# New instruction orders for a one-layer vision transformer on one core

## The reference

```python
h = layernorm(p, ln1_g, ln1_b)                         # p: patches, 1152 x 768
h = layernorm(einsum('bsd,dm->bsm', h, W) + b, ln2_g, ln2_b)   # 192 wide
# attention: 12 heads of 16; each of the 36 patch positions attends over the 32 images
q, k, v = split(norm(h) @ in_proj_weight.T + in_proj_bias)
o = softmax(normalize(q) @ normalize(k).T * exp(min(logit_scale, 4.605))) @ v
h = h + (o * head_scale) @ out_w.T + out_b
# gated FFN with 8-bit activations and 3-valued weights
up, gate = split(bitlinear(norm(h), w_in, g_in))        # 512 each
h = h + bitlinear(silu(gate) * up, w_out, g_out)
```

## Time and profile before

| | |
|---|---|
| median of three runs | 125.61 us (125.09 to 126.04) |
| profiled execution | 125.35 us |
| its span, first to last instruction | 123.5 us |
| busy in the span: PE, DVE, ACT, POOL | 114.8, 104.6, 78.9, 74.6 us |
| mean granted TensorE clock | 0.993 of full speed |
| DMA | 7.68 MB, nearly all of it in the first 35 us |

### The profile page before, as it was taken

One profiled execution on the slowest core, in us unless ns is written; L12 is line 12 of the kernel. 1 busy time (PEld: TensorE's weight loads), 2 busy tenths in 40 slices (PEclk: granted clock), 3 DMA queues, 4 the chain that ended last, 5 costly groups with the idle time before them and its releaser, 6 DMA issues.

```text
span 123.5 us, 4889 instructions
## 1 busy us (share of the span) xinstructions
PE 114.8 (93%) x1940; PEld 95.3 (77%) x1948; DVE 104.6 (85%) x338; ACT 78.9 (64%) x179; POOL 74.6 (60%) x172
## 2 busy tenths in 40 slices
PE   6999999999999998999999979999999999999970
PEld 6989998797997986887867748599686787687850
DVE  0488984899999999799997999999999999998820
ACT  0405356676898555692856948678679587999730
POOL 7100167555446451193782777998887999999800
PEclk9999999999999999999999999999999999999997
DMA  3999978899910000000000000000000000111111
GB/s 90 255 194 178 182 140 163 150 180 222 310 53 0 5 0 5 5 0 5 3 5 0 5 0 5 0 5 5 0 5 3 5 0 16 47 43 53 48 50 49
DMA packets 24509, 7.68 MB, mean 62 GB/s; under 512 B 20579, under 2 KB 23909, under 8 KB 24486
## 3 DMA queue, kind: packets, MB, share of 16 engines
q1 hardware_dynamic: 21732, 6.92, 26.7%
q10 hardware_dynamic: 2754, 0.45, 2.6%
HBM read 6.48 MB, written 0.88 MB: 60 GB/s over the span
## 4 chain that ended last, share of the span: by engine, by line
PE 65%; POOL 10%; DVE 10%; issue 5%; ACT 5%; DVEq 0%; POOLq 0%
PE bank L750 11%; PE bank L772 8%; PE bank L773 7%; PE bank L796 6%; PE bank L784 5%; PE bank L650 4%; PE bank L654 3%; POOL yw L449 3%; PE bank L730 2%; PE bank L761 2%; PE bank L813 2%; PE bank L668 2%; PE bank L814 2%; PE bank L661 2%; PE bank L830 2%
## 5 line engine op out<-in xcount | busy, mean ns | idle before, releaser
L750 PE MATMUL bank<-w_emb_c,xT 128*128 128x192 f32 x108 | 19.3, 329 | 0.0
L654 PE MATMUL bank<-ones 128*128 128x128 f32 x126 | 19.2, 284 | 0.0
L750 PEld LDWEIGHTS bank<-w_emb_c,xT 128*128 128x128 f32 x108 | 17.3, 190 | 0.2
L654 PEld LDWEIGHTS bank<-ones 128*128 128x128 f32 x126 | 16.2, 191 | 1.0 <-issue 0.9
L381 POOL TENSOR_TENSOR rs<-mv,mhalf 128x1 f32<-128x1 f32 x9 | 5.2, 586 | 15.3 <-DVE mv L957 15.3
L772 PE MATMUL bank<-w_qkv,xhT 97*128 97x384 f32 (+1 forms) x36 | 12.0, 415 | 0.9 <-DVE qkp L1026 0.8
L773 PE MATMUL bank<-w_qkv,xhT 96*128 96x384 f32 (+1 forms) x36 | 11.7, 405 | 0.0
L449 POOL TENSOR_TENSOR yw<-yy,gout_bc 128x512 f32<-128x512 f32 x8 | 10.2, 1270 | 0.2 <-POOL yy L438 0.2
L796 PEld LDWEIGHTS bank<-vx,pT 32*32 32x32 f32 x864 | 8.5, 104 | 2.1 <-issue 1.9
L796 PE MATMUL bank<-vx,pT 32*32 32x17 f32 x864 | 9.3, 181 | 0.8 <-issue 0.8
L772 PEld LDWEIGHTS bank<-w_qkv,xhT 97*128 97x128 f32 x36 | 6.2, 189 | 4.1 <-issue 1.6
(11 more groups left out here) (173 smaller groups left out, 336.5 us busy)
## 6 DMA issues: line engine op xcount, KB each, us to landing
xs<-in_x_dram SPq DMA_DIRECT2D x32, 96.0 KB, 3.5
out_dram<-h_all SPq DMA_DIRECT2D x34, 24.0 KB, 1.5
wi_raw<-in_L_ffn_w_in_dram SPq DMA_DIRECT2D x1, 768.0 KB, 6.4
w_emb_sb<-in_L_tok_W_dram SPq DMA_DIRECT2D x2, 288.0 KB, 3.3
w_qkv_raw<-attn_in_proj_weight_dram SPq DMA_DIRECT2D x1, 432.0 KB
xs<-in_x_dram ACTq DMA_DIRECT2D x4, 96.0 KB, 5.0
wo_raw<-in_L_ffn_w_out_dram SPq DMA_DIRECT2D x1, 384.0 KB, 5.0
gout_bc<-in_L_ffn_g_out_dram SPq DMA_DIRECT2D x1, 256.0 KB, 7.6
```

What stands on the lines that cost most here:

```text
L654: nc.tensor.matmul(bank[b][:, 3 * P:4 * P], ones[:, :], ones[:, :], start=True, stop=True)
L750: mm = nc.tensor.matmul(emb_bank, xT[:, t % 3, P * k:P * (k + 1)], w_emb_c[:, 3 * (k % 2) + k // 2, :], start=(k == 0), stop=(k == KF - 1))
```

## The change

Four of the five orders are written anew: GpSimd's, ScalarE's, TensorE's and VectorE's lists; SyncE's stays. The same steps run as before, with these exceptions: tile 4's up part goes by upc(4) on ScalarE and yyp(4) on GpSimd in place of yy_(4) on VectorE; tile 7's weighting is ywd(7) on VectorE in place of yw_(7) on GpSimd; 60 spare calls in place of 63; some extra waits of calls are named differently, and ms2_ loses its own. Diff lines that only reorder steps of which nothing below speaks are left out.

```diff
@@ -46,10 +46,10 @@
...
-WEIGHED_ON_DVE = (8,)
-WEIGHED_ON_POOL = (0, 1, 2, 3, 4, 5, 6, 7)
-UP_COPIED = (0, 1, 2, 3)
-UP_READ = (4, 5, 6, 7, 8)
+WEIGHED_ON_DVE = (7, 8)
+WEIGHED_ON_POOL = (0, 1, 2, 3, 4, 5, 6)
+UP_COPIED = (0, 1, 2, 3, 4)
+UP_READ = (5, 6, 7, 8)
@@ -467,18 +467,18 @@
...
-nw_(4); nv_(4); an4_(0); an4_(1); wfac_(); f_h_(0); rs3_(6); f_h_(1); rs3_(7); rs2_(8); nm3_(6); hg_(8); nw_(5)
-nv_(5); rs3_(8); e5_(0); yyp(0); yw_(0); s4_(2); s4_(3); nm3_(7); nm3_(8); an4_(2); nw_(6); nv_(6); e5_(1)
-f_h_(2); an4_(3); e5_(2); ms5_(0); yyp(1); f_h_(3); yw_(1); s5_(0); an5_(0); yyp(2); ms5_(1); s5_(1); nw_(7)
-nv_(7); ms5_(2); s5_(2); s4_(4); yw_(2); an5_(1); s4_(5); yyp(3); f2_(0); an5_(2); an4_(4); f_h_(4); f2_(1)
-nw_(8); nv_(8); s4_(6); an4_(5); f_h_(5); e5_(3); ms5_(3); e5_(4); e5_(5); yw_(3); s5_(3); an4_(6); yw_(4)
-f2_(2); an5_(3); ms5_(4); f_h_(6); yw_(5); f2_(3); s5_(4); ms5_(5); s4_(7); e5_(6); s5_(5); an4_(7); f_h_(7)
-yw_(6, (yq_ok, 4)); s4_(8); ms5_(6); s5_(6); an4_(8); an5_(4); e5_(7); f2_(4); f_h_(8); yw_(7); ms5_(7); s5_(7)
-an5_(5); f2_(5); e5_(8); an5_(6); an5_(7); f2_(6); f2_(7); ms5_(8); s5_(8); an5_(8); f2_(8)
...
+nv_(4); wfac_(); f_h_(0); rs3_(6); nm3_(6); s4_(1); s4_(2); rs3_(7); nm3_(7); nw_(5); nv_(5); e5_(0); an4_(1)
+f_h_(1); yyp(0); an4_(2); rs2_(8); hg_(8); f_h_(2); e5_(1); s4_(3); nw_(6); nv_(6); yw_(0); yyp(1); yw_(1)
+e5_(2); ms5_(0); s5_(0); an5_(0); f2_(0); rs3_(8); nm3_(8); nw_(7); nv_(7); ms5_(1); s5_(1); an5_(1); an4_(3)
+f_h_(3); e5_(3); yyp(2); s4_(4); s4_(5); yw_(2); an4_(4); an4_(5); f2_(1); f_h_(4); f_h_(5); nw_(8); ms5_(2)
+nv_(8); e5_(4); s5_(2); e5_(5); yyp(3); s4_(6); yw_(3); yyp(4); yw_(4); an4_(6); f_h_(6); ms5_(3); yw_(5)
+s5_(3); ms5_(4); s5_(4); s4_(7); an5_(2); an5_(3); f2_(2); an5_(4); an4_(7); f2_(3); ms5_(5); f2_(4); f_h_(7)
+s4_(8); s5_(5); yw_(6, (yq_ok, 4)); an4_(8); e5_(6); ms5_(6); an5_(5); s5_(6); e5_(7); f2_(5); f_h_(8); ms5_(7)
+s5_(7); an5_(6); an5_(7); f2_(6); e5_(8); ms5_(8); s5_(8); f2_(7); an5_(8); f2_(8)
@@ -556,11 +556,10 @@
...
-def ms2_(t, *freed):
+def ms2_(t):
...
-    wait_all(act, freed)
@@ -624,19 +623,19 @@
...
-xp0(1); xp0(0); xp0(2); xTel(0); xTeh(0); xTel(1); xTeh(1); ms2_(0); xTel(2); xTeh(2); ms2_(1); qkvE_()
-xhTe(0); lse_(); xp_(3); xp_(4); sq_(0); xTel(3); xTeh(3); xhTe(1); xTel(4); xp_(5); vx_(0); ms2_(2); xTel(5)
-ms2_(3, (ms2_ok, 3)); xTeh(4); xTeh(5); sq_(1); woEp_(); xp_(6); vx_(1); xp_(7); xp_(8); xTel(6); xh_(3)
-xhTe(2); absi_(); ms2_(4); pr_(0); vx_(2); xTeh(6); sq_(2); ms2_(5, (ms2_ok, 5)); abso_(); xhTe(3); oTe(0)
...
-sq_(8); xq_(4); ysq_(3); xqTe(4); xq_(5); yq_(1); pr_(7); xqTe(5); vx_(8); yqTe(1); th_(4); yq_(2); xq_(6)
-th_(5); pr_(8); oTe(7); ysq_(4); ysq_(5, (ysq_ok, 5)); xqTe(6); yqTe(2); th_(6); oTe(8); yq_(3); xq_(7); yq_(4)
...
+xp0(1); xp0(0); xp0(2); xTel(0); xTeh(0); xTeh(1); xTel(1); xTel(2); ms2_(0); xTeh(2); ms2_(1); qkvE_(); xp_(3)
+xhTe(0); lse_(); xp_(4); ms2_(2); xTel(3); sq_(0); xTeh(3); xp_(5); vx_(0); xTel(4); xhTe(1); xTeh(4); xTel(5)
+ms2_(3); vx_(1); sq_(1); xTeh(5); woEp_(); xp_(6); xp_(7); ms2_(4); xhTe(2); absi_(); abso_(); pr_(0); xh_(3)
+sq_(2); vx_(2); xTel(6); ms2_(5); xTeh(6); xhTe(3); pr_(1); xp_(8); vx_(3); sq_(3); oTe(0); xh_(4); xTel(7)
...
+xqTe(5); pr_(7); th_(4); yq_(2); upc(4); yqTe(1); ysq_(3); th_(5); oTe(7); pr_(8); xq_(6); ysq_(4); xqTe(6)
+yqTe(2); ysq_(5, (ysq_ok, 5)); th_(6); oTe(8); yq_(3); xq_(7); yq_(4); xqTe(7); yqTe(3); ysq_(6); th_(7)
+yqTe(4); yq_(5); xq_(8); ysq_(7); xqTe(8); yqTe(5); yq_(6); th_(8); yqTe(6); yq_(7); ysq_(8); yqTe(7); yq_(8)
@@ -847,29 +846,29 @@
...
-spare(7); spare(7); xTh(0); spare(7); xTl(1, (xTl_ok, 1)); emb(0); xTh(1); xTl(2, (xTl_ok, 2)); spare(4)
-xTh(2, (xTh_ok, 2)); emb(1, (h0s_ok, 1)); qkvT_(); xhT_(0, (xTh_ok, 3)); emb(2); qkv(0); xTl(3); xTh(3)
-woTp_(); xTl(4, (xTl_ok, 4)); xhT_(1, (xTh_ok, 4)); emb(3); xTh(4, (xhT_ok, 2)); xTl(5)
-qkv(1, (qkn_ok, 1), (vx_ok, 1)); xTh(5, (xTh_ok, 5)); emb(4); sc(0, (p_oE, 1)); xhT_(2); xTl(6)
-emb(5, (h0s_ok, 5)); xTh(6, (xhT_ok, 3)); qkv(2, (qkn_ok, 2)); sc(1); pv(0, (vx_ok, 3)); xhT_(3, (xTh_ok, 7))
-emb(6); oT_(0, (xhT_ok, 4)); xTl(7); wsum_(); proj(0, (sm_ok, 2)); xTh(7); qkv(3, (qkn_ok, 3))
-sc(2, (h2_ok, 1)); xhT_(4); pv(1, (vx_ok, 4)); emb(7); oT_(1, (xhT_ok, 5)); pv(2); proj(1); xTl(8); xTh(8)
-sc(3, (h2_ok, 2)); qkv(4, (on_ok, 3)); oT_(2, (xTh_ok, 9)); wiT_(); emb(8); pv(3, (vx_ok, 5)); xqT_(0); xhT_(5)
-proj(2); ff1(0); qkv(5, (on_ok, 4)); oT_(3); sc(4); woT_((yg_ok, 1)); spare(7); spare(7); spare(7); xqT_(1)
-xhT_(6); proj(3, (sm_ok, 5)); ff1(1); qkv(6, (qkn_ok, 6)); spare(7); spare(7); spare(7); spare(7)
-pv(4, (vx_ok, 7)); xhT_(7); xqT_(2); sc(5); ff1(2, (yg_ok, 2)); oT_(4); qkv(7, (qkn_ok, 7)); sc(6)
-pv(5, (vx_ok, 8)); spare(7); spare(7); proj(4, (sm_ok, 7)); oT_(5); xqT_(3); pv(6); xhT_(8, (oT_ok, 6))
-proj(5, (h2_ok, 5)); spare(7); oT_(6, (xhT_ok, 9)); ff1(3); yqT_(0); proj(6, (h2_ok, 6)); qkv(8, (qkn_ok, 8))
-sc(7, (h2_ok, 7)); xqT_(4); spare(7); spare(7); spare(7); spare(7); spare(7); xqT_(5); spare(7); spare(7)
-yqT_(1); spare(7); spare(7); ff1(4, (xqT_ok, 6)); pv(7, (vx_ok, 9)); spare(7); sc(8); ff2(0)
-ff1(5, (yy_ok, 1)); spare(4); oT_(7); spare(4); spare(4); spare(4); spare(4); spare(4); proj(7); yqT_(2)
...
-spare(4); ff2(5, (out_ok, 5)); spare(4); spare(4); spare(4); yqT_(6); spare(4); spare(4); spare(4); spare(4)
-ff2(6, (out_ok, 6)); yqT_(7); spare(4); spare(4); spare(4); spare(4); ff2(7, (out_ok, 7)); spare(4); spare(4)
-spare(4); yqT_(8); spare(4); spare(4); spare(7, (out_ok, 8)); spare(7); ff2(8)
...
+xTh(0); spare(7); spare(7); xTl(1, (xTl_ok, 1)); spare(7); xTh(1, (xTh_ok, 1)); emb(0); xTl(2, (xTl_ok, 2))
+xTh(2); emb(1, (h0s_ok, 1)); qkvT_(); emb(2, (h0s_ok, 2)); xhT_(0); xTl(3); qkv(0); xTh(3); xTl(4, (xTl_ok, 4))
+woTp_(); xhT_(1, (xTh_ok, 4)); emb(3); xTl(5, (xTl_ok, 5)); xTh(4, (xhT_ok, 2)); qkv(1, (qkn_ok, 1))
+xTh(5, (xTh_ok, 5)); emb(4, (h0s_ok, 4)); sc(0, (p_oE, 1)); xhT_(2); emb(5, (h0s_ok, 5)); qkv(2, (qkn_ok, 2))
+xTl(6); sc(1); xTh(6); pv(0, (vx_ok, 3)); xhT_(3, (xTh_ok, 7)); emb(6); qkv(3, (qkn_ok, 3)); xTl(7); oT_(0)
+pv(1, (vx_ok, 4)); proj(0); xTh(7); wsum_(); xTl(8, (xTl_ok, 8)); xhT_(4, (xTh_ok, 8)); sc(2, (h2_ok, 1))
+oT_(1, (xhT_ok, 5)); emb(7); proj(1, (sm_ok, 3)); pv(2); xTh(8); sc(3, (h2_ok, 2)); qkv(4, (on_ok, 3))
+oT_(2, (xTh_ok, 9)); wiT_(); pv(3, (vx_ok, 5)); xhT_(5); proj(2); xqT_(0, (p_wiE, 2)); oT_(3, (xhT_ok, 6))
+qkv(5, (qkn_ok, 5)); ff1(0); sc(4); emb(8); xhT_(6); proj(3, (sm_ok, 5)); xqT_(1); woT_(); qkv(6, (qkn_ok, 6))
+ff1(1, (p_woE, 1)); xhT_(7); spare(7); pv(4, (vx_ok, 7)); spare(7); xqT_(2, (up_ok, 2)); sc(5)
+ff1(2, (yg_ok, 2)); qkv(7, (qkn_ok, 7)); sc(6); oT_(4); pv(5, (vx_ok, 8)); spare(7); spare(7)
+proj(4, (sm_ok, 7)); oT_(5); xqT_(3); pv(6); xhT_(8, (oT_ok, 6)); proj(5, (h2_ok, 5)); ff1(3, (yg_ok, 3))
+oT_(6, (xhT_ok, 9)); qkv(8, (qkn_ok, 8)); yqT_(0); proj(6, (h2_ok, 6)); spare(7); spare(7); spare(7)
+sc(7, (h2_ok, 7)); xqT_(4); spare(7); spare(7); spare(7); xqT_(5, (xqT_ok, 5)); yqT_(1); spare(7); spare(7)
+ff1(4, (xqT_ok, 6)); ff2(0); pv(7); sc(8); spare(4); spare(4); spare(4); ff1(5, (yg_ok, 5), (up_ok, 5))
...
+spare(7, (out_ok, 5)); ff1(8); ff2(5); spare(4); yqT_(6); spare(4); spare(4); spare(4); spare(4)
+ff2(6, (out_ok, 6)); spare(4); yqT_(7); spare(4); spare(4); spare(4); spare(4); ff2(7, (out_ok, 7)); spare(4)
+spare(4); spare(4); spare(4); spare(4); yqT_(8); spare(7, (out_ok, 8)); spare(7); spare(7); spare(7); ff2(8)
@@ -1099,7 +1098,7 @@
...
-    if t == 8:
+    if t == WEIGHED_ON_DVE[0]:
@@ -1130,32 +1129,32 @@
...
-qs4_(1); qkn_(4); rsum_(3); on_(3); kT_(4); h2_(2); qT_(4); bst4_(2); yg_(0); h_(8); mv4_(2); bst3_(8); xc_(2)
-ss_(5); mv3_(8); ssm_(5); ng_(5); mx_(4); sm_(4); np0_(5); np1_(5); np2_(5); np3_(5); qkn_(5); ax4_(2); h2_(3)
-pT_(4); qT_(5); bst4_(3); mv4_(3); kT_(5); xc_(3); ri4_(2); ax4_(3); qs4_(2); ss_(6); ssm_(6); ng_(6); yg_(1)
-rsum_(4); ri4_(3); np0_(6); np1_(6); np2_(6); qs4_(3); np3_(6); on_(4); qkn_(6); mx_(5); qT_(6); sm_(5); kT_(6)
-yg_(2); pT_(5); ax5_(0); mx_(6); ri5_(0); sm_(6); rsum_(5); ss_(7); on_(5); pT_(6); ssm_(7); h2_(4); ng_(7)
-qs5_(0); ax5_(1); bst4_(4); np0_(7); rsum_(6); mv4_(4); np1_(7); on_(6); np2_(7); xc_(4); np3_(7); ri5_(1)
...
-qs4_(7); yy_(6); out_(1); h2_(8); ax5_(5); bst4_(8); ri5_(5); mv4_(8); out_(2); xc_(8); qs5_(5); ax4_(8)
-ri4_(8); qs4_(8); yg_(7); yy_(7); out_(3); ax5_(6); ri5_(6); out_(4); qs5_(6); ax5_(7); ri5_(7); qs5_(7)
-yg_(8); out_(5); yy_(8); ywd(8); ax5_(8); out_(6); ri5_(8); qs5_(8); out_(7); out_(8)
...
+bst4_(2); kT_(4); mv4_(2); ri4_(1); qT_(4); xc_(2); mv3_(7); ax4_(2); ss_(5); qs4_(1); ssm_(5); mx_(4); ng_(5)
+yg_(0); sm_(4); np0_(5); ri4_(2); np1_(5); np2_(5); np3_(5); qs4_(2); qkn_(5); h0s_(8); h2_(3); pT_(4)
+bst4_(3); kT_(5); qT_(5); mv4_(3); xc_(3); h_(8); ax4_(3); ss_(6); ssm_(6); ri4_(3); ng_(6); bst3_(8); yg_(1)
+np0_(6); rsum_(4); np1_(6); qs4_(3); np2_(6); mv3_(8); np3_(6); on_(4); qkn_(6); mx_(5); qT_(6); sm_(5); kT_(6)
```

(34 more changed lines are left out.)

49 lines of the change are left out of this document (20 added, 29 removed).

## The result

The changed kernel is 1% slower: median 126.83 us over 18 executions, against 125.57 us over 18 of the kernel before; the ratio is 1.0099, 95% interval 1.0064 to 1.0134. (Seven of the 18 executions, with a mean granted clock of 0.93 to 0.99, took 128.4 to 132.8 us; the ratio leaves them out.) The profiled execution took 125.62 us with a span of 123.8, and is the fastest of the 18.

What follows compares the result with a forecast made beforehand. TensorE was taken to set the pace up to qkv(6), VectorE to 113 us, then the last tile's chain. -3.5 + 0.7 + 2.4 + 0.5 - 0.3 = -0.2 us on 125.35, plus 0.26: 125.4 us, range 122.2 to 127.6.

Steps and rivals of the forecast that it cites:

- the main mechanism: GpSimd's wide operations hold the shared SBUF ports and stop VectorE's 24-column operations, costing most of what TensorE's order gains.
- tile 6: Behind nv_(6), GpSimd's yw_(0), yyp(1), yw_(1) stop VectorE's np operations: two blocks, +2.4 us; bounds nothing to 3.4.
- the swap: yy_(4) to ScalarE and GpSimd, yw_(7) to VectorE: even on VectorE and GpSimd, hidden on ScalarE, 0 us.
- the lists behind tile 6: After qkn(6), VectorE as full as before and yg(8) near 113 us; no separate loss forecast.
- Stage B: First emb to qkv(6), TensorE's order: fewer spares, ff1(1) later, stop and wait gone; -3.5 us at qkn(5).
- VectorE's list: h0s(8), h(8) and tile 8's statistics now follow qkn(5), tile 2's ax4 goes the other way: +0.7 us.
- rival 3: TensorE's stop without visible cause comes again, in pv(2) and sc(3) or elsewhere: 0.8 us more, 126.2 us; chance 0.10.
- Tiles 5 and 8: GpSimd's yyp(0) may stop np3(5) and yyp(3) may stop np3(8) on VectorE: together +0.5 us.
- Rival 2: Slower: wide operations catch tiles 5 and 8 too, with tile 6 at its full 3.4 us: 128.2 us; chance 0.15.
- Stage D: Last 10.5 us, the last tile's chain: f2(7) now behind s5(8), no longer ahead of ms5(8): -0.3 us.
- Behind out_(8): End of the run: no DMA moved and the queue of stores as it was, so 0 us.

Runs made afterwards that it cites:

- experiment 8: Changed kernel with the swap undone (yy_(4) back on VectorE, yw_(7) back on GpSimd): 128.1 us, 1.0217 of the kernel before.
- experiment 10: Changed kernel with the three spare matmul calls between sc(8) and ff1(5) moved behind ff1(5): 127.55 us, 1.0128 of the kernel before.
- experiment 2: Changed kernel with yyp(1) and yw_(1) moved behind GpSimd's small operations at tile 6, yw_(0) left in place: 124.88 us, 0.99 of the kernel before.
- experiment 1: Changed kernel with yw_(0), yyp(1) and yw_(1) moved behind GpSimd's small operations at tile 6: 124.34 us, 0.9882 of the kernel before.
- experiment 12: Changed kernel with experiment 1's edit and yyp(2), yg_(2) and upc(2) moved earlier: 124.12 us, 0.9863 of the kernel before.
- experiment 3: Kernel before with yyp(1) and yw_(1) moved up directly behind nv_(6) on GpSimd: 127.11 us, 1.0148 of the kernel before.
- experiment 5: Kernel before with the whole swap alone (upc(4) and yyp(4) for yy_(4), ywd(7) for yw_(7)): 126.74 us, 1.0105 of the kernel before.
- experiment 6: Kernel before with the up half of the swap alone (upc(4) and yyp(4) for yy_(4)): 126.72 us, 1.0071 of the kernel before.
- experiment 7: Kernel before with the weighting half of the swap alone (ywd(7) for yw_(7)): 125.74 us, 0.9996 of the kernel before.
- experiment 11: Changed kernel with experiment 1's edit, experiment 10's edit, and xp_(3) and xTl(3) put back as before: 124.35 us, 0.9866 of the kernel before.
- experiment 13: Changed kernel with two fill matmuls replaced by 48 small ones, shifting TensorE's later code: 130.31 us, 1.0338 of the kernel before.
- experiment 14: Changed kernel with experiment 1's edit and four fill matmuls replaced by 96 small ones, shifting TensorE's later code: 144.13 us, 1.1467 of the kernel before.

## Why the prediction was wrong

It said 125.4 us, 0.2 less than before; the ratio of 1.0099 makes it some 1.2 us more. The range held the time and the main mechanism was the right one, but the sign was not, since gain and loss were of one size and terms were off. Two of them turned the sign: tile 6, too small by 0.6 us, and the swap and the lists behind tile 6, put at nothing, where 1.16 us were lost. That the sum of the profiled execution comes out near the forecast is in part luck, since misses on both sides cancel.

- *Stage B, -3.5, and VectorE's list, +0.7:* -3.5 forecast at qkn_(5), -2.60 there in the profiled execution; +0.7 forecast behind it, +0.17 by ssm_(6). The sum, -2.43 for -2.8, fits better than its parts. qkv(6), at 69.65, came just outside the 68 to 69.5 that were to show it. np3_(5), 1.31 us before, takes 0.18 after, which alone is 1.1 us; I had put 0.8 there. The 0.79 us of the stop in pv(1) did not go: it came again as 0.86 in pv(2) and 0.42 in pv(4), as rival 3 had it. And the profiled execution is a lucky one: of five other kernels with the same lists up to there, three (experiments 8, 10 and 2) have the end of qkn_(5) at 71.13, 69.29 and 71.54 us, and two (1 and 12), in executions with some 14 us at 1.2 GHz, at 76.58 and 76.59, while four with the lists of before (3, 5, 6 and 7) have it at 72.18, 71.99, 72.04 and 72.68.
- *Tile 6, +2.4:* right in mechanism and place, wrong in size. Three operations were stopped, not two: 0.95 + 0.98 + 0.95 = 2.9 us of excess, and 3.0 us on the path. Experiments 1, 2 and 3 show it by taking it away, by leaving a third, and by putting it into the other kernel.
- *Tiles 5 and 8, +0.5:* nothing came of it. Rival 2, the slower one, had these two as its condition; its sign came, not its mechanism.
- *The swap, 0:* the step that failed. "Even on VectorE and GpSimd" compared busy times, 0.67 against 0.69 and 1.27 against 1.27. What counts is where they stand. yy_(4) stood ahead of a wait, so its removal gave nothing; yyp(4) stands ahead of yw_(4), on an engine 36.01 of 40.80 us busy in that stage. In the old lists the whole swap costs 1.05%, and its up half alone 0.7%. In the new lists it can't be priced by undoing it, because yw_(7) then comes too late on GpSimd. There, from qkn_(6) to yg_(8), 1.16 us are lost that I had at nothing, and yg_(8), which was to stay near 113, starts at 114.77. Between yy_(6) and yg_(8) VectorE's list has ywd(7), 0.69, and out_(5), 0.41, more and out_(1), 0.41, less, and it waits 0.5 us longer for GpSimd: 0.17, 0.41 and 0.30 us for s5_(5) to s5_(7), against 0.18 for yw_(7) and 0.21 for s5_(7) before. yg_(5) also comes 0.53 us later behind qkn_(8), waiting 0.58 for th_(5), but the stretch from qkn_(6) to qkn_(8) had given 0.51 us back. How much of GpSimd's lateness is yyp(4) and how much its new order stays open.
- *Stage D, -0.3:* from yg_(8) to out_(8) 5.85 us in place of 6.28. Two things changed there: out_(5), 0.41, left VectorE's list, and ms5_(8) follows the end of ysq_(8) by 0.11 us in place of 0.32, with f2_(7) gone from ahead of it. qs5_(8) needs both sides, and they came together (ri5_(8) ended at 118.01 us, s5_(8) at 117.94), so f2_(7) alone can't have given the 0.3; no run tells the two apart.
- *Behind out_(8), 0:* 2.5 us in place of 3.5 in the profiled execution. I had taken this as unchanged.

By the profiled execution the sum is -2.60 + 0.17 + 3.00 + 1.16 - 0.43 - 1.05 = +0.25. That the ratio says 1.2 is in part the spread of stage B; the rest stays open, as does what shortens the end behind out_(8), since taking stores off SyncE did not.

## What to carry to other kernels

Ahead of moving an operation on VectorE or GpSimd, write down what stands beside it on the other of the two: here a 0.18 us operation beside a 1.27 us one cost 0.95 us each time, and moving one small operation between them gave 0.74 us on the path and 1.4% in time. Such a gap is only as wide as the lists are punctual, as experiment 11 shows. Two engines' busy times that balance say nothing on a swap: ask of each removed operation what the next one waits for, and of each added one who waits for what is queued behind it. A profile of one execution is one draw: the fastest of 18 showed +0.25 us where the ratio says 1.2.

## What the runs showed of the hardware

- *TensorE's stops go with transfers of its code.* The traces of all 17 kernels have 34 stops of over 0.3 us without another cause within pv or sc; each ended 2.2 to 2.9 us after a transfer of 16 KB on the instruction queue had begun. That TensorE waits for the code is inferred from this and from experiments 13 and 14. In the two kernels of the prediction they came where TensorE ran through 191 to 227 recorded instructions in the 2.3 us behind such a start; where it ran through up to 136 there was none, and in one place with 208 none either, so this is no threshold. The Trainium skill (Runtime: NRT & Kernel Launch, "Instruction fetch mechanics") calls the cost of such a refill mostly hidden; if the stops are that cost, it was up to 2.71 us at a time here.
- *The clock fell behind some of these stops.* In experiment 14 the stops of 1.43, 2.48 and 2.71 us ended at 46.4, 56.7 and 98.5 us; in the stretches from 47.3, 57.6 and 98.5 us on TensorE was granted 1.2 GHz, between them 2.4 (first fence). In experiment 1 a stop of 1.40 us ended at 56.2 us, and 1.2 GHz held from 57.6 to 71.2 (second). In all 17 traces, between 40 us and the last 10 us of the span, the clock fell eleven times: ten times at the end of such a stop or up to 1.6 us behind it, once behind a wait of 2.01 us for qkn_(6) (experiment 10). But behind 24 of the 34 stops it did not fall, one of 1.45 us in experiment 14 among them, and in experiment 2 it fell behind one of 0.86. The columns are those of the earlier trace rows:

```profile
16.60:47.00 30.40, 28.74 (x358) 25.16 (x357) 25.17 (x79) 19.61 (x50) 16.19 (x35) 1.00 0.53 117
47.30:50.50 3.20, 3.20 (x12) 3.20 (x11) 3.10 (x12) 1.28 (x3) 0.81 (x2) 0.50 0.00 0
...
57.60:64.10 6.50, 6.50 (x70) 5.86 (x69) 4.26 (x18) 2.49 (x7) 0.55 (x1) 0.50 0.01 3
...
98.50:101.70 3.20, 2.98 (x10) 1.90 (x11) 2.19 (x9) 1.79 (x3) 0.60 (x2) 0.50 0.00 0
```

```profile
57.60:71.20 13.60, 13.60 (x137) 9.47 (x138) 9.20 (x34) 6.35 (x12) 6.08 (x15) 0.50 0.01 2
```
